# Five groups of the first gather and five of the seventh wait for TensorE's work

## The reference

```python
x = _layernorm(x + _L0_gnn_ref(x, edge_attr_48, src, dst, eps))   # relu(x[src] + e), summed by dst
x = _layernorm(x + _L1_gnn_ref(x, src, dst, W, b))                # x[src] * rsqrt(out_deg[src]), summed by dst, matrix
x = _layernorm(x + _L2_gnn_ref(x, edge_index, W, b))              # sqrt-normalized x[dst], summed by src, matrix
x = _layernorm(x + _L3_gnn_ref(x, edge_index, edge_attr_40, ...)) # gated x[dst], summed by src, layer norm
```

## Time and profile before

| | |
|---|---|
| three runs, us | 3155.09, 3162.78 (median), 3171.98 |
| profiled execution: its own time, its span | 3144.17, 3142.4 |
| busy: PE, PEld, DVE, ACT, POOL | 615.5, 488.1, 1940.1, 643.1, 1776.5 us |
| mean granted TensorE clock | 0.541 of full speed |
| chain that ended last, by engine | DVE 38%, issue 26%, another core or an unknown queue 16%, ACT 7%, PE 7%, POOL 5% |

### The profile page before, as it was taken

One profiled execution on the slowest core, in us unless ns is written; L12 is line 12 of the kernel. 1 busy time (PEld: TensorE's weight loads), 2 busy tenths in 40 slices (PEclk: granted clock), 3 DMA queues, 4 the chain that ended last, 5 costly groups with the idle time before them and its releaser, 6 DMA issues.

```text
span 3142.4 us, 12819 instructions
## 1 busy us (share of the span) xinstructions
PE 615.5 (20%) x2850; PEld 488.1 (16%) x2850; DVE 1940.1 (62%) x2769; ACT 643.1 (20%) x1141; POOL 1776.5 (57%) x1768
## 2 busy tenths in 40 slices
PE   1112500000277544554331000011023000000000
PEld 0000200000266444443331000010023000000000
DVE  2001899988776546655538289930026999998863
ACT  1002600221233222111111223310001113232110
POOL 5773004774555553765677776677723305564776
PEclk8555855555565555665555555555555555555555
DMA  3110194885134223221000444421111112220000
GB/s 115 22 21 10 48 331 165 314 295 213 30 119 147 94 89 101 65 57 31 14 17 20 170 118 141 142 76 29 19 33 34 67 57 80 82 75 26 17 17 14
DMA packets 110179, 276.20 MB, mean 88 GB/s; under 512 B 38521, under 2 KB 63427, under 8 KB 109971
## 3 DMA queue, kind: packets, MB, share of 16 engines
q1 hardware_dynamic: 46371, 196.46, 17.3%
q0 software_dynamic: 56448, 44.23, 7.5%
q10 hardware_dynamic: 7280, 34.67, 3.0%
HBM read 142.41 MB, written 138.17 MB: 89 GB/s over the span
## 4 chain that ended last, share of the span: by engine, by line
DVE 38%; issue 26%; another core or an unknown queue 16%; ACT 7%; PE 7%; POOL 5%; DMA 1%; SPq 0%; DVEq 0%; ACTq 0%; POOLq 0%
PE PS L930 4%; DVE PS L1382 3%; DVE var L1391 3%; POOL x_table L519 3%; DVE du L1385 3%; PE PS L916 2%; POOL ring L462 2%; DVE sumb L1308 2%; ACT sq L610 1%; DVE do L1402 1%; ACT GX L667 1%; DVE do L1151 1%; DVE MG L1375 1%; DVE GX L1404 1%
## 5 line engine op out<-in xcount | busy, mean ns | idle before, releaser
L505 POOL DMA_INDIRECT ring<-h_by_src,zs x196 | 206.6, 1054 | 330.5 <-ACTq L851 179.8
L475 POOL DMA_INDIRECT XD<-xa_table,dstI x196 | 187.7, 958 | 289.5 <-SPq L370 230.1
L462 POOL DMA_INDIRECT ring<-x_with_degree,srcI x196 | 208.2, 1062 | 149.4 <-DVEq L1466 87.8
L519 POOL DMA_INDIRECT x_with_degree<-sumb,put x196 | 195.7, 998 | 169.8 <-ACTq L691 113.4
L610 ACT ACTIVATE sq<-du 128x1344 f32<-128x1344 f32 x128 | 167.7, 1321 | 561.8 <-DVE du L1385 437.4
L519 POOL DMA_INDIRECT x_table<-sumb,put x196 | 214.1, 1093 | 90.6 <-issue 59.4
L519 POOL DMA_INDIRECT out<-sumb,put x196 | 195.1, 996 | 98.4 <-issue 60.9
L475 POOL DMA_INDIRECT XD<-in_xaux,srcI x196 | 188.9, 964 | 85.8 <-issue 59.5
L462 POOL DMA_INDIRECT ring<-edge_records,dstI x196 | 187.5, 957 | 84.7 <-issue 58.6
L1278 DVE TENSOR_SCALAR GX<-GX 128x784 bf16<-128x784 int16 x196 | 75.0, 428 | 252.8 <-remote 211.1
L475 POOL DMA_INDIRECT XD<-x_table,srcI x196 | 192.3, 981 | 59.8 <-issue 59.8
(11 more groups left out here) (295 smaller groups left out, 2668.9 us busy)
## 6 DMA issues: line engine op xcount, KB each, us to landing
din<-in_xaux SPq DMA_DIRECT2D x56, 728.0 KB
xa_table<-din SPq DMA_DIRECT2D x28, 728.0 KB
x_table<-GX SPq DMA_DIRECT2D x28, 686.0 KB
x_with_degree<-GX SPq DMA_DIRECT2D x28, 686.0 KB
din<-x_table SPq DMA_DIRECT2D x28, 686.0 KB
x_table<-do SPq DMA_DIRECT2D x28, 672.0 KB
din<-x_table SPq DMA_DIRECT2D x28, 672.0 KB
out<-do SPq DMA_DIRECT2D x28, 672.0 KB
```

Source lines behind the costliest of these rows:

```text
L462: pool.indirect_dma_start(ring[:, h, t, 0:w], None, table, bass.IndirectOffsetOnAxis(ap=of[:, c * H + t:c * H + t + 1], axis=0), **skip).t ...
L475: pool.indirect_dma_start(XD[:, t, 0:w], None, table, bass.IndirectOffsetOnAxis(ap=of[:, t:t + 1], axis=0)).then_inc(rows[c].sem, rows[c]. ...
L505: pool.indirect_dma_start(ring4[:, c % 4, t, :], None, H2, bass.IndirectOffsetOnAxis(ap=of[:, c * H + t:c * H + t + 1], axis=0), bounds_ch ...
L519: pool.indirect_dma_start(table, bass.IndirectOffsetOnAxis(ap=put[:, c * H + t:c * H + t + 1], axis=0), rows_of[:, h, t, :], None, bounds_ ...
```

## The change

POOL gets up to five waits within two of the gathers. In the first, group 1 waits until `counted` is 14, so 10 columns are counted, and groups 2, 3, 4 and 5 wait for 50, 92, 134 and 176 columns. Groups 6 to 13 follow with no wait. In the seventh, groups 4, 6, 8, 10 and 12 wait until 2, 4, 5, 6 and 7 blocks of h2 are made. No transfer, operand or other wait changes. The second gather, the third call of the same function, is as before.

```diff
+COUNTED = {1: 4 + 10, 2: 4 + 50, 3: 4 + 92, 4: 4 + 134, 5: 4 + 176}
+H2_DONE = {4: 2, 6: 4, 8: 5, 10: 6, 12: NBLK}
...
-            def gather_in_place(table, w, of, free=None):
+            def gather_in_place(table, w, of, free=None, behind=None, pace={}):
 
                 for c in range(CE // H):
+                    if c in pace:
+                        pool.wait_ge(S[behind], pace[c])
                     if free:
                         pool.wait_ge(free.sem, free.up())
...
-            gather_in_place(A["xaux"], XW, srcI)
+            gather_in_place(A["xaux"], XW, srcI, behind="counted", pace=COUNTED)
...
-            gather_in_place(X2, D, srcI)
+            gather_in_place(X2, D, srcI, behind="h2_ready", pace=H2_DONE)
```

## The result

Five runs of the changed kernel took 3070.98 to 3087.49 us, median 3082.97, against 3162.78 for the kernel before; the ratio is 0.9756, with an interval of 0.9721 to 0.979. The forecast was 2985 us and 178 us of gain. The profiled execution has a span of 3069.2 us.

A forecast was written before the change was run, and what follows sets the result against it. DVE was taken to wait for PE completions arriving late while POOL issues gathers 1 and 7. Gains of 128 us (gather 1) and 50 us (h2) sum to 178: 3162.8 - 178 = 2985 us, range 2925 to 3090.

The forecast's parts named there:

- What is late is the arrival of completions, and a matmul pair costs 2.8 us: Beside gathers 1 and 7: PE's completions arrive late, 2.8 us per PE instruction as counted in the code, 5.6 us a column.
- A backlog of 1.4 us per transfer: POOL's row gathers: each transfer leaves 1.4 us to be worked off, while POOL issues one per 1.25 to 1.28 us.
- The count ends at 230: Column count beside gather 1: with the waits it ends at 230 us, 135 us earlier; bounds 219 and 308.
- an allowance of 4 us for DVE's turns beside gather 1: DVE's 14 turns beside gather 1: 4 us lost, because their instructions share SBUF with POOL's for some 90 us.
- the 11.5 us for each turn: DVE's 14 turns after the count: some 160 us, 11.5 each, from 254 to near 404.
- -128 forecast for gather 1: Waits of gather 1: count 135 us earlier, less 3 us for PE flips and 4 for DVE's turns, net 128 us gained.
- What is queued behind is gather 2, which waits for xa_done anyway: Behind the delayed gather 1: gather 2 waits until about 380 anyway, leaving 30 us and more to spare.
- from there to gather 7 DVE's chain is shifted whole: From DVE's first rows of gather 2 to gather 7: the chain moves forward whole, keeping gather 1's gain.
- h2, -50 us: Blocks of h2 beside gather 7: the waits gain 50 us, between estimates of 55.6 and 41.
- The port as cause: One-hots beside POOL's issuing: a DVE and GpSimd port lock as another cause of 5.6 us a column; trace judged against it.
- Rival D: Whole kernel: stalls belong to the profiled execution alone, so timed runs stay at 3163 us; chance 0.05.
- rival B: Port rule: 3 columns a group, the rest at once, count ends at 299, h2 gains about 55; 3046 us, chance 0.09.

The follow-up runs named there:

- the third experiment: The changed kernel with the second gather also held back until DVE's 14 turns and sort are done; ratio 0.9395 to the kernel before, 2971 us.
- the pairs: Kernel before, without the change's waits, plus two POOL memsets after every second transfer of gathers 1 and 7; ratio 0.8699, 2751 us.
- the spaced kernel: Kernel before, without the change's waits, plus a small POOL memset, waited for, after each transfer of gathers 1 and 7; ratio 0.8653, 2737 us.

## Why the prediction was wrong

- *What is late is the arrival of completions, and a matmul pair costs 2.8 us*: right, and more general than I put it: 1.4 us for each instruction of PE and of DVE.
- *A backlog of 1.4 us per transfer*: right to a microsecond in three places that were not used to fit it (342.0, 499.5, and in gather 7: 2050.8 + 84 x 1.4 = 2168.4, first block made at 2169.0). Spacing clearly above 1.4 us removes it; between 1.396 (late) and 1.49 us nothing was measured on a chip that shows the lateness. While it builds up the rule is less exact (below), and the run with every second transfer spaced doesn't follow it in size.
- *The count ends at 230*: it ended at 175.5. The steps between groups took 29 to 31 us instead of 34, and the last 20 columns 9 us instead of 37 or more, because in the first us of a group PE was faster than I allowed. The timeline of the last columns, beside group 5 (from 166.35):

```profile
170.61 1.51 DVE L1282 TENSOR_SCALAR GX<-GX 128x784 bf16<-128x784 int16 x4 [0.40 <-PE PS L978]
...
174.94 0.56 DVE L1282 TENSOR_SCALAR GX<-GX 128x784 bf16<-128x784 int16 x1 [0.99 <-PE PS L978]
```

Columns come every 0.46 us until 173 and some 17 one-hots start in 8.6 us, where I counted 14 columns in 10. The prompt time is no longer than I took from rows 6: after 7 to 8 us in each group most columns are 1.4 us or more apart.
- **The step that failed: "an allowance of 4 us for DVE's turns beside gather 1", and the 11.5 us for each turn on which the rest of the gather 1 sum stood.** The turns took 356 us from first to last start instead of 148. That only PE's completions are late I had from a stretch in which nothing else could be seen to be. But in the kernel before DVE has one instruction in 5.6 us there and could not show it: with a limit of one completion per 1.4 us it is never the late one. A turn is some 9 comparisons and as many other short instructions, each waiting for the one before, and in the kernel before they ran in the only long stretch in which POOL had nothing to issue. Bringing the count forward by 189 us pushed them out of it. Term by term: -128 forecast for gather 1; measured were +33 at the start of gather 7 in the first profile, +12 there with +11 in the ratio on the first chip of the experiments, and -2 on the fourth. The count's gain is real, and the turns spend all of it.
- *What is queued behind is gather 2, which waits for xa_done anyway; "from there to gather 7 DVE's chain is shifted whole"*: the table too came earlier, so gather 2 began at 330.8, 2.3 us after gather 1, and lay on the turns as well (80 instructions in 112 us, above). I had seen that it would come forward and priced its effect on the turns at nothing; held back, it gives 85 to 114 us.
- *h2, -50 us*: right in kind, too small in size: -100 in the first profile, -82 and -80 in those of two other chips. The first two blocks were forecast 102 us after the start and came at 98 (2183.6). Behind the pause of 26.8 us, though, the blocks beside POOL took 16, 26 and 21 us and not 42 + 14.6. Only block 6, beside 56 unbroken transfers, was slow (60.5 us), and it came free at the moment that 2225.7 + 56 x 1.4 = 2304.1 gives.
- *The port as cause*: out, as forecast; DVE is late without POOL writing (window 440 to 455, and 327 to 342 in the third experiment), and its durations don't change. By the lock that the Trainium skill describes ("SBUF — State Buffer", Who interferes with whom), held for the whole of an instruction by the engine that came first, DVE would have gone on once POOL stopped. The trace doesn't agree.
- *Rival D, only the profiled execution*: out. The medians fell as the spans did: 80 and 73 us here, 411 and 416 for the pairs on the fourth chip. Whether the other timed executions write the same records as the profiled one no run tells. What is left behind by a transfer, and what accepts the completions, no run here shows; the Trainium skill's rule on records that push back ("NOTIFIC — the notification-queue block", Overflow: three behaviours, one of which stalls the engine) would fit the shape, and stays untested. Open too is why one chip of those used doesn't have it.
- Two small sums of the prediction are off, with no weight in the outcome: by its own figures rival B's count ends at 47 + 4 x 35.5 + 20 x 5.6 = 301 and not 299, and 163.6 us for 14 turns are 11.7 each.

## What to carry to other kernels

Before a stretch of work is moved forward, ask what *else* moves, and into whose company: an engine that showed no waits beside a busy neighbour may simply have had too few instructions to be held up. Where completions arrive at a fixed beat, count instructions per engine, not microseconds, and look for the source of the beat: here one small memset per transfer, on an engine that made up 5% of the chain that ended last, gained 13%, over five times what stopping that engine in chosen places gave. And repeat such a finding on a second chip before building on it: on one of those used here the same memsets cost 1 to 2%.

## What the runs showed of the hardware

- Row transfers issued by POOL 1.26 to 1.40 us apart hold the completions of PE and of DVE to one per 1.4 us each, for as long as 1.4 us times their number; starts come on a beat of 0.7 us (240.62, 242.72, 246.23, 249.03, 251.12, 252.52). At an average of 1.49 us (gather 7 of the spaced kernel, after its first block) and of 1.55 us nothing is late; at 1.396 us a column still takes 4.2 us.
- After a rest the lateness sets in only after a while: PE after 11 us or 7 to 8 us (the groups of gather 1 in the changed kernel), DVE not within 40 us (89 instructions between 504 and 544, with 30 transfers). That the two differ so isn't explained by a common backlog.
- A transfer of 64 rows costs POOL 0.91 us against 0.95 for 128, and leaves as much behind.
- One chip of the four in these calls took 2538 us for the kernel that takes 3143 to 3172 on the other three.
